# FFN chunks in two-bank tiles of the scan's PSUM ring, and two PSUM banks for the out-projection

## The chip, the cores and the metric

One Trainium2 chip, 8 cores. Each core runs the same program on one of 8 batch rows, with no exchange between cores. The metric is the device time of the slowest core, in microseconds; lower is better. A verdict takes a median over several executions.

## The reference

Per batch row: x is [4096, 1024]. It is normalised, goes through a two-directional state-space scan (16 heads of 128, state 64, a causal convolution of 4 taps before it), and the sum of both directions is projected back; beside it an FFN product with block-quantised operands and a silu gates the result.

```python
xn = _layernorm(x)
zxbcdt = xn @ in_proj_w.T
y_fw = _branch(zxbcdt, ...)                       # conv + silu, SSD scan, * silu(z), rms norm
y_bw = _branch(zxbcdt[:, ::-1, :], ...)
s = (y_fw + y_bw[:, ::-1, :]) @ out_proj_w.T
xq, xs = _mx_quantize(xn); wq, ws = _mx_quantize(weight)    # blocks of 32
g = _silu((xq * xs) @ (wq * ws).T + bias)
x = x + s * g
```

## The kernel before

The row of 4096 tokens is cut into 16 groups of 256 tokens, and a group into 2 chunks of 128. The kernel makes two passes. The first goes through the groups backwards: it projects, runs the backward scan and spills x, B and C, silu(z), y and the quantised xn (sp_x, sp_bc, sp_z, sp_y, sp_xd) to memory. The second, which this change touches, goes forwards and for each group g does:

- `b_scan(g)`: the scan of both chunks, written by `scan_pair`. `weights` makes the decay exponents in a two-bank PSUM tile (TensorE, `ps<-rh,lts`), takes exp of 1024 columns on ScalarE and two products on VectorE (`e`). `outputs` makes y (`ps<-xtm,e`, then `ps<-st,gc`), which VectorE gates with silu(z) (`yz<-ps,sz`). `carry` makes the new state (`ps<-xtm,bw`, then `st`). `factors` makes `gc` and `dec` from the broadcast decays `g`. `norm` makes the rms factor in small operations and scales yz.
- `decays(g + 1)`: the small decay sums of the next group, with the matmuls `ps<-sm,tri` and `ps<-sm,onesf` (one of each a group), a transpose `ltt<-spl`, a store `scr<-ltt` and the loads `rh<-scr` and `g<-scr`.
- `b_out(g - 1, ...)`: the out-projection of the two chunks of the group before; each chunk is two halves of 512 columns, each half two units of 8 matmuls (`ps<-ar,yt`, or `ps<-ar` where the transposed yz lies in `ar`). VectorE multiplies by the FFN gate (`ost<-ps,ar` or `ar<-ps,ar`), GpSimd adds the residual.
- `b_sum(g)`: yz plus the backward y (`yz<-yz,ar` or `yz<-yz,yb`), then its transposes (`yt<-yz`, or `ar<-yz`).
- `b_front(g + 1)`: loads, and `conv_group`, which runs the convolution on TensorE (`ps<-sbc,cd` once and `ps<-stg,cd` x32 for each of four quarters, in one two-bank tile CV), silu on ScalarE (`cvb`, `cvx` x4), the transposes `xtm<-cvx`, and the small product `ps<-cvb` in a tile of PJ.
- `ffn_chunk` for the two chunks of group g: for each half of 512 columns 8 matmuls `ps<-ar,xt` and one for the bias (`ps<-ar,on`), then a silu into gf (`ar<-ps` on ScalarE).

PSUM has 8 banks of 512 columns: `PJ` two of one bank, `CV` one of two banks, `SC` two of two banks. A `Ring` hands its buffers out in turn, in the order in which the code asks; whoever takes one waits for the last reader. Before this change the second pass splits PJ: bank 0 is PO (out-projection), bank 1 is PF (FFN halves and the small product).

The order in which each engine works is not that of the code. `Plan.queues` simulates the program with costs of its own and always picks, among the units of an engine that are ready, the one of lowest rank (its turn). A unit's waits stand before it, but on TensorE `emit` moves a wait that was known early into the last matmuls of the unit ahead (the last four of a short unit, the last two of a long one), so that unit ends late if the awaited thing is late. ScalarE takes its table functions in order of turn: all exp of a turn, then all silu of the next, so there are two table loads a group. Reordering thus follows from any change of rings or costs.

Of the kernel before, what the change touches and what calls it, by code (L numbers as in the profile page):

```python
# [12 lines left out]
AF = mybir.ActivationFunctionType  # L13
# [30 lines left out]
def flat(tokens):  # L44
    for t in tokens:
        if t is None:
            continue
        if isinstance(t, (list, tuple)):
            yield from flat(t)
        else:  # L50
            yield t


class Plan:
# [8 lines left out]
    def put(self, eng, steps, after, us, table=None):  # L63
        if not isinstance(steps, list):
            steps = [steps]
        rank = self.turn if self.rank is None else self.rank
        land = 0.25 if eng == "pe" else 0.12
        self.units.append(Unit(eng, steps, sorted(set(flat(after))), us, land, table, None,
                               self.turn, rank))
        return len(self.units) - 1  # L70

    def dma(self, eng, slot, step, after, kb, us=0.5, rate=180.0, lat=None):
        land = lat or 2.0 + kb / rate
        rank = self.turn if self.rank is None else self.rank
        self.units.append(Unit(eng, [step], sorted(set(flat(after))), us, land, None, slot,
                               self.turn, rank))
        return len(self.units) - 1
# [119 lines left out]
def pe_us(cols):  # L197
    return cols / 2300.0


def act_us(n):
    return 0.18 + n * 0.00083


def dve1(n):
    return 0.16 + n * 0.00104
# [50 lines left out]
def record(nc, dr, A, PS):  # L257
    P = Plan()
    put, dma = P.put, P.dma
# [10 lines left out]
    on3 = A("on3", [128, 128], BF16)  # L270
# [48 lines left out]
    ps = PS("ps", [128, 4096], F32)  # L319
# [9 lines left out]
    PJ = Ring("pj", [ps[:, 0:512], ps[:, 512:1024]])  # L329
    CV = Ring("cv", [ps[:, 1024:2048]])  # L330
    SC = Ring("sc", [ps[:, 2048:3072], ps[:, 3072:4096]])
# [34 lines left out]
    def mm(out, lhsT, rhs, start, stop):  # L366
        return lambda e: e.matmul(out, lhsT, rhs, start=start, stop=stop)  # L367

    def act(out, in_, func, bias=None, scale=None, accum=None):
        kw = {}  # L370
        if bias is not None:
            kw["bias"] = bias
        if scale is not None:
            kw["scale"] = scale
        if accum is not None:
            kw["accum_out"] = accum
        return lambda e: e.activation(out, in_, func, **kw)  # L377

    def tt(out, a, b, op):
        return lambda e: e.tensor_tensor(out, a, b, op=op)  # L380
# [12 lines left out]
    def go(out, in_, **kw):  # L393
        return lambda e: e.dma_start(out=out, in_=in_, **kw)  # L394
# [44 lines left out]
    k_on3 = dma("sp", "k3", go(on3[:], dr["c_on3"]), [k_wz[3]], 32)  # L439
# [626 lines left out]
    for q in range(4):  # L1066
# [18 lines left out]
    wfv = ar[:, WF:WF + 8192].rearrange("p (m k f) -> p m k f", m=8, k=8)  # L1085
    k_wf = dma("sp", "wfl", go(wfv, dr["wf"].rearrange("m p k f -> p m k f")),
               [old, wf_stores], 2048)
# [6 lines left out]
    fbt = ar[:, fb_o:fb_o + 1024]  # L1094
    z_fb = put("pool", lambda e: e.memset(fbt, 0.0), [old], 0.9)
    k_fbt = dma("sp", "k15", go(fbt[0:3, :], dr["fbd"]), [k_fbd, z_fb], 6)
# [6 lines left out]
    for r in (YT, YB, GF):  # L1103
        for i in range(len(r.bufs)):
            r.free[i] = [last_a["wx"]]
    XD = Ring("xdl", [xt[i // 2][:].rearrange("p k t -> p (k t)")[
        :, i % 2 * 1024:(i % 2 + 1) * 1024].rearrange("p (k t) -> p k t", k=8) for i in range(4)])
# [9 lines left out]
    def ffn_chunk(ci):  # L1117
        di, xd_, dfree = XD.take()
        h = dma("sp", f"xdl{di}", go(xd_, dr["sp_xd"][ci]),
                [dfree, spill[ci // 2]["xd"][1 - ci % 2]], 256)  # L1120
        gi, gf, gfree = GF.take()
        evs, ps_ = [], []
        for nh in range(2):
            pi, pj, pfree = PJ.take()
            steps = [mm(pj, xd_[:, k, :], wfv[:, nh * 4:(nh + 1) * 4, k, :], k == 0, False)
                     for k in range(8)]
            steps.append(mm(pj, on3[:], fbt[:, nh * 512:(nh + 1) * 512], False, True))
            p = put("pe", steps, [h, k_wf, k_fbt, k_on3, pfree], pe_us(9 * 512))
            ps_.append(p)
            a = put("act", act(gf[:, nh * 512:(nh + 1) * 512], pj, AF.Silu), [p, gfree],  # L1130
                    act_us(512), table="silu")
            PJ.give(pi, [a])
            evs.append(a)
        XD.give(di, ps_)
        return {"g": (gi, gf, evs)}

    def b_front(g):
# [57 lines left out]
    def b_out(g, sc, ff, c):  # L1195
# [6 lines left out]
        for nh in range(2):  # L1202
            hs_ = slice(nh * 512, (nh + 1) * 512)
            pi, pj, pfree = PO.take()
            p = None
# [6 lines left out]
            m = put("dve", tt(o[:, 0:512], pj, gf[:, hs_], ALU.mult), [p, t_g, ofree], dve1(512))  # L1212
            PO.give(pi, [m])
            mu.append(m)
# [6 lines left out]
        U.give(ui, [t_o])  # L1221
        GF.give(gi, mu)

    PO = Ring("po", [ps[:, 0:512]])
    PF = Ring("pf", [ps[:, 512:1024]])
    PO.free, PF.free = [PJ.free[0]], [PJ.free[1]]
    PJ.bufs, PJ.free, PJ.n = PF.bufs, PF.free, 0
    base = P.turn
    P.rank = base - 0.5
    dcs = {0: decays(0, None, t_par, None)}  # L1230
# [19 lines left out]
    for g in range(NG):  # L1250
        P.turn = base + 2 * g + 2
        front["dc"] = dcs[g]
        scans = b_scan(g, front)
        free_group(front, scans)
        if g < NG - 1:
            P.rank = P.turn - 0.5
            dcs[g + 1] = decays(g + 1, None, t_par, None)
            P.rank = None
        if g:
            for c in range(2):  # L1260
                b_out(g - 1, old_scans[c], ffs[c], c)
        b_sum(g, scans)
        old_scans = scans
        P.turn += 1
        if g < NG - 1:
            front = b_front(g + 1)
        ffs = [ffn_chunk(2 * g + c) for c in range(2)]
# [5 lines left out]
def build_nc():  # L1273
# [27 lines left out]
    def PS(name, shape, dt):  # L1301
        return nc.psum_tensor(name, shape, dt).__enter__()

    plan = record(nc, dr, A, PS)
    order = plan.queues()
    count = plan.count
# [85 lines left out]
```

How the kernel before makes its waits and increments, by code:

```python
    def emit(self, eng, handle, sems, queue):  # L156
        units = [self.units[i] for i in queue]
        early = [[] for _ in units]
        if eng == "pe":
            for n in range(1, len(units)):
                if len(units[n - 1].steps) > 4:
                    early[n - 1] = [w for w in units[n].waits if w[2] < units[n - 1].value]
        for n, u in enumerate(units):
            for w in u.waits:
                if not n or w not in early[n - 1]:
                    handle.wait_ge(sems[w[0]], w[1])
            for k, step in enumerate(u.steps):
                if k == len(u.steps) - (4 if u.us < 1.2 else 2):
                    for w in early[n]:
                        handle.wait_ge(sems[w[0]], w[1])
                last = step(handle)
            last.then_inc(sems[u.slot or u.eng], 16 if u.slot else 1)
# [1136 lines left out]
        @block.sync  # L1311
        def _(eng):
            plan.emit("sp", eng, sems, order["sp"])
            for name, value in count.items():
                eng.wait_ge(sems[name], value)
```

## Time and profile before

| | |
|---|---|
| median of 3 runs | 1570.39 us (1562.2 to 1576.58) |
| profiled execution, its own time | 1570.03 us |
| span of its slowest core (core 3) | 1568.1 us; the others 1537.6 to 1566.1 |
| PE busy | 1280.4 us, 82% of the span |
| VectorE, ScalarE, GpSimd busy | 1051.2, 826.2, 709.7 us (67, 53, 45%) |
| mean granted clock of core 3 | 0.949 |
| chain that ended last | PE 46%, DMA 21%, ACT 11%, issue 9%, DVE 6%, SPq 4% |

Times in the rows are microseconds from the start of the span. PE is TensorE, DVE VectorE, ACT ScalarE, POOL GpSimd, SPq the queue of SyncE, which issues all DMAs of the second pass. A bracket at the end of a row gives the idle time of the engine ahead of it and what ended it. Almost all operations are recorded by one helper line each (matmul L367, activation L377), so the names of the tiles tell them apart. The second pass runs from about 850 us to the end.

### The profile page before, as it was taken

Reading aid. Unit: us, or ns where it says so; the run is one execution under the profiler, and the core shown is the slowest. Engines: PE = TensorE matmul, PEld = TensorE weight load, DVE = VectorE, ACT = ScalarE, POOL = GpSimd, SP = SyncE. Lnnn points to the kernel's source line nnn. Section 1 sums busy time; section 2 is a strip of 40 time slices with the busy share of each in tenths; the row PEclk is TensorE's granted clock in tenths of the full one; section 3 lists DMA queues with packets and bytes.
Section 4 is the critical chain, followed back from the end, with each engine's and each line's share of the span. In section 5 each row is a group of like instructions: output and inputs, shape, how many; then the busy total and the mean of one; then the engine's idle time right before and its main releaser. Section 6 shows DMA issues by size and latency. Waiting matters only on the chain.

```text
span 1568.1 us, 38096 instructions; the slowest of 8 cores (1537.6 to 1568.1 us)
## 1 busy us (share of the span) xinstructions
PE 1280.4 (82%) x13440; PEld 774.8 (49%) x13440; DVE 1051.2 (67%) x1792; ACT 826.2 (53%) x1660; POOL 709.7 (45%) x950
## 2 busy tenths in 40 slices
PE   0577898876998899999996579888888888888896
PEld 0453665553666666666663344444444444444442
DVE  2635788655778887788754776567766667776662
ACT  0225566454566566666664664455555555555541
POOL 2332566534545556665531434444434444343443
PEclk9888999988999999999997599999999999999999
DMA  9793788999777988877679878888878889888872
GB/s 170 133 185 90 177 212 192 142 214 182 162 179 182 200 194 195 167 161 167 176 195 234 209 174 218 220 186 202 213 182 216 203 213 209 201 220 208 201 181 85
DMA packets 434548, 291.92 MB, mean 186 GB/s; under 512 B 312687, under 2 KB 383087, under 8 KB 432826
## 3 DMA queue, kind: packets, MB, share of 16 engines
q1 hardware_dynamic: 431770, 276.62, 76.0%
q0 software_dynamic: 2592, 12.88, 5.2%
q8 instruction: 109, 1.79, 0.5%
q14 instruction: 77, 0.63, 0.2%
HBM read 149.20 MB, written 83.89 MB: 149 GB/s over the span
## 4 chain that ended last, share of the span: by engine, by line
PE 46%; DMA 21%; ACT 11%; issue 9%; DVE 6%; SPq 4%; POOL 0%; DVEq 0%; ACTq 0%; POOLq 0%
PE ps L367 46%; DMA xtm<-cvx 5%; SPq L394 4%; DMA g<-scr 4%; DMA scr<-ltt 3%; ACT L377 3%; DMA xt<-xn 2%; ACT cvx L377 2%; DMA ltt<-spl 2%; ACT e L377 2%; DMA ar<-yz 2%; DVE yz L380 1%; DMA rh<-scr 1%; DMA yt<-yz 1%; ACT ar L377 1%
## 5 line engine op out<-in xcount | busy, mean ns | idle before, releaser
L367 PE MATMUL ps<-ar,xt 128*128 128x512 bf16 (+1 forms) x1792 | 382.8, 358 | 123.9 <-DMA xt<-xn 44.3
L367 PEld LDWEIGHTS ps<-ar,xt 128*128 128x128 bf16 x1792 | 150.4, 99 | 317.7 <-issue 174.3
L367 PE MATMUL ps<-xt,ar 128*128 128x256 bf16 x2176 | 267.2, 279 | 25.5 <-ACT cvx L377 11.1
L377 ACT ACTIVATE cvx<-ps,cbt 128x256 bf16<-128x256 f32 x512 | 200.6, 474 | 164.4 <-PE ps L367 99.5
L380 POOL TENSOR_TENSOR stmp<-st,dec 128x1024 f32<-128x1024 bf16 x64 | 132.0, 2062 | 257.8 <-DVE st L380 113.0
L367 PEld LDWEIGHTS ps<-xt,ar 128*128 128x128 bf16 x2176 | 210.4, 100 | 65.4 <-issue 32.4
L380 DVE TENSOR_TENSOR yz<-ps,sz 128x1024 bf16<-128x1024 f32 x128 | 156.2, 1220 | 48.6 <-PE ps L367 48.1
L377 ACT ACTIVATE sq<-yz 128x1024 bf16<-128x1024 bf16 x128 | 134.9, 1054 | 83.6 <-DVE yz L380 58.4
L367 PE MATMUL ps<-ar 128*128 128x512 bf16 x704 | 167.8, 380 | 10.4 <-DVE rr L384 4.3
L367 PE MATMUL ps<-stg,cd 64*64 64x256 bf16 x4096 | 149.7, 285 | 23.9 <-DMA xt<-xn 6.6
L385 POOL TENSOR_SCALAR rr<-rr 128x1 f32<-128x1 f32 x384 | 120.0, 318 | 86.5 <-DVE rr L385 51.1
L380 DVE TENSOR_TENSOR e<-e,cbm 128x1024 bf16<-128x1024 bf16 x128 | 103.3, 810 | 83.1 <-ACT e L377 80.2
L377 ACT ACTIVATE e<-ps 128x1024 bf16<-128x1024 f32 x128 | 129.7, 1017 | 31.8 <-PE ps L367 31.3
L367 PEld LDWEIGHTS ps<-stg,cd 64*64 64x64 bf16 x4096 | 109.7, 111 | 73.1 <-issue 69.7
L380 POOL TENSOR_TENSOR bw<-btm,w 128x1024 bf16<-128x1024 bf16 x64 | 125.7, 1966 | 42.4 <-DMA btm<-cvb 24.5
L377 ACT ACTIVATE sz<-ps 128x512 bf16<-128x512 f32 x128 | 76.5, 598 | 106.2 <-PE ps L367 105.5
L380 POOL TENSOR_TENSOR xd<-v,qs 128x1024 bf16<-128x1024 fp8e4 x40 | 86.7, 2167 | 98.4 <-DVE v L865 41.6
L367 PE MATMUL ps<-xtm,e 128*128 128x128 bf16 x1024 | 85.0, 226 | 52.1 <-DVE spl L391 17.8
L384 POOL TENSOR_SCALAR u<-u,stats 128x1024 f32<-128x1024 f32 x32 | 93.2, 2913 | 71.3 <-DVE xn L385 30.8
L377 ACT ACTIVATE stg<-ps 128x512 bf16<-128x512 f32 x128 | 75.5, 593 | 86.0 <-PE ps L367 85.4
L367 PEld LDWEIGHTS ps<-ar 128*128 128x128 bf16 x704 | 64.0, 98 | 90.0 <-issue 25.0
L377 ACT ACTIVATE ar<-ps 128x512 bf16<-128x512 f32 x64 | 38.4, 600 | 129.2 <-PE ps L367 114.5
(97 smaller groups left out, 1869.1 us busy)
## 6 DMA issues: line engine op xcount, KB each, us to landing
u<-u SPq DMA_DIRECT2D x54, 512.0 KB, 5.6
sp_x<-stg SPq DMA_DIRECT2D x64, 256.0 KB, 3.1
g<-scr SPq DMA_DIRECT2D x64, 256.0 KB, 5.6
sp_z<-sz SPq DMA_DIRECT2D x32, 512.0 KB, 3.6
sp_y<-yz SPq DMA_DIRECT2D x32, 512.0 KB, 4.7
sz<-sp_z SPq DMA_DIRECT2D x32, 512.0 KB, 4.9
stg<-sp_x SPq DMA_DIRECT2D x60, 259.0 KB, 5.9
out<-u SPq DMA_DIRECT2D x22, 512.0 KB, 3.6
```

Of the source, the lines that this page charges most:

```text
L367: return lambda e: e.matmul(out, lhsT, rhs, start=start, stop=stop)
L377: return lambda e: e.activation(out, in_, func, **kw)
L380: return lambda e: e.tensor_tensor(out, a, b, op=op)
L384: return lambda e: e.tensor_scalar(out, a, s1, None, op0=op0)
L385: return lambda e: e.tensor_scalar(out, a, s1, s2, op0=op0, op1=op1)
L394: return lambda e: e.dma_start(out=out, in_=in_, **kw)
```

## The change

In `ffn_chunk` both halves of a chunk go into one two-bank tile taken from SC, the ring of the scan; one silu of 1024 columns reads it and frees it, where two silus of 512 each freed a bank of PF. A scan takes 10 tiles of SC and a group's two FFN chunks now 2, between the carry of the group's second chunk and the first `weights` of the next group's scan. PF is gone: PO is now PJ itself, so the out-projection has both banks in turn, shared with the small product of `conv_group`.

```diff
         gi, gf, gfree = GF.take()
-        evs, ps_ = [], []
+        si, sp, sfree = SC.take()
+        p = None
         for nh in range(2):
-            pi, pj, pfree = PJ.take()
-            steps = [mm(pj, xd_[:, k, :], wfv[:, nh * 4:(nh + 1) * 4, k, :], k == 0, False)
+            half = sp[:, nh * 512:(nh + 1) * 512]
+            steps = [mm(half, xd_[:, k, :], wfv[:, nh * 4:(nh + 1) * 4, k, :], k == 0, False)
                      for k in range(8)]
-            steps.append(mm(pj, on3[:], fbt[:, nh * 512:(nh + 1) * 512], False, True))
-            p = put("pe", steps, [h, k_wf, k_fbt, k_on3, pfree], pe_us(9 * 512))
-            ps_.append(p)
-            a = put("act", act(gf[:, nh * 512:(nh + 1) * 512], pj, AF.Silu), [p, gfree],
-                    act_us(512), table="silu")
-            PJ.give(pi, [a])
-            evs.append(a)
-        XD.give(di, ps_)
+            steps.append(mm(half, on3[:], fbt[:, nh * 512:(nh + 1) * 512], False, True))
+            p = put("pe", steps, [h, k_wf, k_fbt, k_on3, sfree, p], pe_us(9 * 512))
+        evs = put("act", act(gf[:], sp, AF.Silu), [p, gfree], act_us(1024), table="silu")
+        SC.give(si, [evs])
+        XD.give(di, p)
...
-    PO = Ring("po", [ps[:, 0:512]])
-    PF = Ring("pf", [ps[:, 512:1024]])
-    PO.free, PF.free = [PJ.free[0]], [PJ.free[1]]
-    PJ.bufs, PJ.free, PJ.n = PF.bufs, PF.free, 0
+    PO = PJ
```

What the planner makes of it. TensorE, end of a group in the middle of the second pass, before. `stg,cd` is a quarter of the convolution, `ar,xt` with `ar,on` an FFN half, `rh,lts` the exponents of the next scan, `ar` alone out-projection:

```order
L367 MATMUL ps<-rh,lts1 128x4x64 x8
L367 MATMUL ps<-ar,xt0 128x512 [waits s_act,s_xdl1]
L367 MATMUL ps<-ar,xt0 128x512 x7
L367 MATMUL ps<-ar,on3 128x512
L367 MATMUL ps<-ar,xt0 128x512 [waits s_act]
L367 MATMUL ps<-ar,xt0 128x512 x6
L367 MATMUL ps<-ar,xt0 128x512 [waits s_yt1]
L367 MATMUL ps<-ar,on3 128x512
L367 MATMUL ps<-ar 128x512 x14
L367 MATMUL ps<-ar 128x512 [waits s_act]
L367 MATMUL ps<-ar 128x512
L367 MATMUL ps<-rh,lts1 128x4x64 x4
```

The same place after, in a group whose next chunk's transposed yz has the semaphore s_yt0:

```order
L367 MATMUL ps<-stg1,cd 64x256 [waits s_act,s_rh]
L367 MATMUL ps<-stg1,cd 64x256 x3
L367 MATMUL ps<-rh,lts0 128x4x64 x4
L367 MATMUL ps<-rh,lts0 128x4x64 [waits s_act]
L367 MATMUL ps<-rh,lts0 128x4x64 x3
L367 MATMUL ps<-stg2,cd 64x256 [waits s_act,s_sxl2]
L367 MATMUL ps<-stg2,cd 64x256 x27
L367 MATMUL ps<-stg2,cd 64x256 [waits s_yt0]
L367 MATMUL ps<-stg2,cd 64x256 x3
L367 MATMUL ps<-ar 128x512 x22
L367 MATMUL ps<-ar 128x512 [waits s_act]
L367 MATMUL ps<-ar 128x512
```

The FFN halves have moved ahead of the last two quarters; the wait for the transposed yz has moved from the last FFN half into the last quarter of the convolution; three units of out-projection follow, where two did. Other groups end otherwise. This is the end of the next one after, up to the decays' matmul sm,tri:

```order
L367 MATMUL ps<-stg2,cd 64x256 x32
L367 MATMUL ps<-ar,xt0 128x512 x8
L367 MATMUL ps<-ar,on3 128x512
L367 MATMUL ps<-rh,lts1 128x4x64 x4
L367 MATMUL ps<-stg3,cd 64x256 x32
L367 MATMUL ps<-ar,xt0 128x512 x8
L367 MATMUL ps<-ar,on3 128x512
L367 MATMUL ps<-rh,lts1 128x4x64 x8
L367 MATMUL ps<-sm0,tri 128x32
L367 MATMUL ps<-sm0,onesf 128x32
L367 MATMUL ps<-xtm1,e0 128x128 x8
```

No out-projection stands between its last quarter and the next scan's first xtm,e. Counted from one sm,tri to the next over the 13 intervals in the middle of the pass, the units of out-projection were 8 each, but 10 in the first; after they are 12, 4, 12, 6, 10, 4, 12, 4, 12, 4, 12, 6 and 10.

VectorE, from the broadcast decays to the sums of yz, before (rr scales: the norm):

```order
L384 TENSOR_SCALAR yz1<-yz1,rr0 128x2048 [waits s_pool]
L380 TENSOR_TENSOR gc0<-g,cvb1 128x1024 [waits s_g01,s_g00]
L380 TENSOR_TENSOR yz1<-yz1,ar 128x2048 [waits s_dve,s_ybl0]
L391 CAST dec0<-g 128x8
L380 TENSOR_TENSOR gc1<-g,cvb1 128x1024
L391 CAST dec1<-g 128x8
L384 TENSOR_SCALAR yz2<-yz2,rr1 128x2048 [waits s_pool]
L380 TENSOR_TENSOR yz2<-yz2,yb 128x2048 [waits s_dve,s_ybl1]
```

and after, as in 9 of those 13 groups:

```order
L380 TENSOR_TENSOR gc0<-g,cvb1 128x1024 [waits s_g01,s_g00]
L391 CAST dec0<-g 128x8
L380 TENSOR_TENSOR gc1<-g,cvb1 128x1024
L391 CAST dec1<-g 128x8
L384 TENSOR_SCALAR yz1<-yz1,rr0 128x2048 [waits s_pool]
L380 TENSOR_TENSOR yz1<-yz1,ar 128x2048 [waits s_dve,s_ybl0]
L384 TENSOR_SCALAR yz2<-yz2,rr1 128x2048 [waits s_pool]
L380 TENSOR_TENSOR yz2<-yz2,yb 128x2048 [waits s_dve,s_ybl1]
```

The first norm and the first sum have moved behind both gc products.

## Rows read from the trace of the kernel before

**Rows 1.** Waits of PE, 880 to 1540: total us, times, longest

```profile
PE ps L367 <- ACT ar L377: 30.0, 26, 2.6
PE ps L367 <- DVE spl L391: 17.8, 12, 1.5
PE ps L367 <- DVE sm L380: 16.1, 17, 2.0
```

**Rows 2.** Chain that ended last, second pass: start, us, what

```profile
969.53 1.28 ACT L377
...
1264.87 1.28 ACT L377
...
1290.11 6.95 DMA g<-scr
...
1299.12 6.66 DMA ar<-yz
...
1471.68 1.28 ACT L377
```

**Rows 3.** Busy by window: us, PE, PEld, DVE, ACT, POOL, PEclk, DMA, GB/s

```profile
1300.00:1400.00 100.00, 84.98 (x831) 44.15 (x830) 70.20 (x111) 52.11 (x102) 39.76 (x55) 1.00 0.92 218
```

**Rows 4.** Timeline of PE, one group: start, us, instruction, wait

```profile
1269.80 0.36 PE L367 MATMUL ps<-sm,tri 128*128 128x32 f32 x2
...
1284.77 0.64 PE L367 MATMUL ps<-xtm,bw 128*64 128x128 bf16 x16
...
1300.37 1.89 PE L367 MATMUL ps<-ar,xt 128*128 128x512 bf16 x8 [0.29 <-ACT ar L377]
...
1303.36 1.67 PE L367 MATMUL ps<-ar,xt 128*128 128x512 bf16 x7 [0.89 <-ACT ar L377]
1305.92 0.38 PE L367 MATMUL ps<-ar,xt 128*128 128x512 bf16 x1 [0.88 <-DMA ar<-yz]
...
1311.72 0.49 PE L367 MATMUL ps<-xtm,e 128*128 128x128 bf16 x6 [0.89 <-DVE sm L380]
```

**Rows 5.** Timeline of DVE, the same group

```profile
1297.22 0.69 DVE L380 TENSOR_TENSOR gc<-g,cvb 128x1024 bf16<-128x1024 bf16 x1 [1.62 <-DMA g<-scr]
...
1301.42 2.46 DVE L384 TENSOR_SCALAR yz<-yz,rr 128x2048 bf16<-128x2048 bf16 x1
```

**Rows 6.** Timeline of ACT, the same group

```profile
1298.06 1.57 ACT L377 ACTIVATE cvx<-ps,cbt 128x256 bf16<-128x256 f32 x4 [1.35 <-DMA xtm<-cvx]
...
1306.61 0.60 ACT L377 ACTIVATE ar<-ps 128x512 bf16<-128x512 f32 x1 [3.39 <-PE ps L367]
1307.22 1.28 ACT L377 ACT_TABLE_LOAD   x1
```

**Rows 7.** Groups by form, 880 to 1540: count, busy, mean ns, idle before

```profile
L377 ACT ACTIVATE e<-ps 128x1024 bf16<-128x1024 f32 x64 | 64.9, 1016 | 28.0 <-PE ps L367 28.0
...
L377 ACT ACTIVATE ar<-ps 128x512 bf16<-128x512 f32 x63 | 37.8, 600 | 126.8 <-PE ps L367 112.1 <-DVE ar L380 11.0 <-DVE rr L385 3.6
```

**Rows 8.** Timeline of PE, the end of the kernel

```profile
1540.19 1.89 PE L367 MATMUL ps<-ar,xt 128*128 128x512 bf16 x8 [1.63 <-ACT ar L377]
...
1546.69 3.61 PE L367 MATMUL ps<-ar 128*128 128x512 bf16 x16 [0.94 <-DVE ost L380]
...
1556.01 3.61 PE L367 MATMUL ps<-ar 128*128 128x512 bf16 x16 [1.08 <-DVE ost L380]
```

**Rows 9.** DMA issues, 880 to 1540: median us to landing

```profile
xtm<-cvx SPq DMA_TRANSPOSE x64, 5.9
```

**Rows 10.** Timeline of SP, which issues the DMAs, the same group

```profile
1304.53 1.57 SPq L394 DMA_TRANSPOSE xtm<-cvx  x1
```

**Rows 11.** Busy by window, a short stretch; PEclk is third from the end

```profile
1130.00:1135.00 5.00, 3.18 (x9) 1.01 (x9) 5.00 (x5) 1.41 (x5) 4.05 (x2) 0.75 1.20 282
```

**Rows 12.** Timeline of PE in that stretch

```profile
1131.62 2.76 PE L367 MATMUL ps<-ar,xt 128*128 128x512 bf16 x8 [1.99 <-ACT ar L377]
...
1135.70 3.57 PE L367 MATMUL ps<-ar,xt 128*128 128x512 bf16 x8 [0.89 <-ACT ar L377]
```

## Prediction

> **What bounds the kernel now.** I read the waits of TensorE first, then the chain that ended last, then TensorE, ScalarE and VectorE in order of time over one group of the second pass. In the second pass TensorE waits most often for ScalarE's silu of an FFN half: 30.0 us in 26 waits [rows 1]. That is the single bank: a half can't start before the silu of the half before has read it. Behind it stand the waits for e at the head of a scan, 17.8 and 16.1 us [rows 1].
>
> These waits are not the whole of the bound. The chain shows a table load for exp at 969.53 and again at 1471.68, twelve groups later: (1471.68 - 969.53) / 12 = 41.85 us for a group [rows 2]. TensorE is busy 84.98 of 100 us [rows 3], so a group holds 41.85 x 0.85 = 35.6 us of its work and 6.3 us of gaps. My marker is the small matmul sm,tri, one per group. From the marker at 1269.80 the group goes on so [rows 4]: carry of the second chunk at 1284.77, then the FFN halves, where the ring costs 0.29 and 0.89 us, then 0.88 us for the transposed yz, which landed at about 1305.8, 36.0 us after the marker; then the next scan's first xtm,e at 1311.72. The chain says why yz is that late: the decays' broadcast g lands at 1290.11 + 6.95 = 1297.1, VectorE's product gc waits for it, the sum of yz stands behind gc in VectorE's queue, and its transposes take 6.66 us more [rows 2, 5]. ScalarE's last silu starts at 1306.61 and the table load at 1307.22, so 1.4 us after yz landed; the marker then follows 4.9 us after a table load (1264.87 to 1269.80) [rows 2, 4, 6]. So the ring and the arrival of yz both end the same stretch, within a microsecond.
>
> **The change, part by part.**
>
> *Two silus of 512 columns become one of 1024.* 0.600 us each before; the same read of 1024 columns with exp takes 1.016 [rows 7]. 1.20 - 1.02 = 0.18 us less on ScalarE for each of 32 chunks, 6 us in all. ScalarE is the waiting side there (its silus wait for PE), so I count nothing. If it counted in full it would be 6 us.
>
> *The waits of the ring go.* At most the 30.0 us of [rows 1]. What makes them vanish also lets all four FFN halves run earlier: they no longer stand behind the third and fourth convolution but ahead of them. What took the time under the last transposes, silus and table load is then gone from there.
>
> *Out-projection in two banks.* In the tail the last 64 matmuls no longer wait for VectorE: three waits, the first 0.94 and the last 1.08 us, together 3.0 us [rows 8]. The wait of 1.63 us of the last FFN half [rows 8] goes too, but yz's transposes may be what comes next there; I take 1 us. Tail: -4 us (bounds 0 and -4.7). With two banks the planner also runs out-projections ahead, and unevenly: counted between markers, the 13 intervals of the middle hold 12, 4, 12, 6, 10, 4, 12, 4, 12, 4, 12, 6 and 10 units of 8 matmuls, where before each held 8. A unit is half of 3.61, 1.8 us [rows 8]. So TensorE's work in an interval is 35.6 + 4 x 1.8 = 42.8, 35.6 - 7.2 = 28.4, 32.0 or 39.2 us.
>
> *What moves onto the path.* In 9 of the 13 intervals (all but those with 4 units) the early wait for yz now stands in the last matmuls of the third or fourth convolution, no longer in the last FFN half. There it holds up a convolution, and with it the last silus before the table load. Also, in 9 of 13 groups both gc products, which wait for g, now stand ahead of the first norm of yz on VectorE, in 2 more one of them; before, the norm was ahead of both. A gc is 0.69 us, the slow norm 2.46 [rows 5]. The nearest bounds for yz's landing: 36.0 us after the marker as before (the norms are often late anyway), and 36.0 + 0.7 + 2.5 = 39.2. I take 37.5, nearer the lower end, since the scan with more out-projections in it makes the norms late rather than g.
>
> Each kind of interval then:
> - 12 units: TensorE reaches the wait after 42.8 - 7.8 = 35.0 us of work (behind it stand 4 units and a decay matmul group, 7.2 + 0.6), plus one scan gap of 1.5 (17.8 / 12, [rows 1]) = 36.5. yz at 37.5; 37.5 + 7.8 = 45.3.
> - 10 units: work reaches the wait sooner, yz decides: 45.3.
> - 6 units: again yz decides: 37.5 + 0.1 for the rest of the convolution + 1.6 of silus [rows 6] = 39.2, + 4.9 to the marker = 44.1.
> - 4 units: no wait for yz, but nothing is left to fill the tail. The last convolution ends after some 27.4 us of work + 1.5 + 0.5 for the single conv tile = 29.4, silus 31.0, marker 35.9. Then the first xtm,e of the next scan needs the transposes of the fourth quarter, which start only now: 5.9 us median [rows 9], 36.9, where before they had been issued ahead of the table load. In the crowded stretch they were issued at 1304.53, which is 34.7 after the marker, and so landed near 40.6 at the latest [rows 4, 9, 10]. Between 36.9 and 40.6, leaning to the free queue, I take 38.2.
>
> Sum: 5 x 45.3 + 2 x 45.3 + 2 x 44.1 + 4 x 38.2 = 558.1 against 13 x 41.85 = 544.1: +14.0. With the tail's -4: +10. The profiled execution took 1570.0 us by its own clock, the median of the runs is 1570.4, so both stand together, and I forecast 1570.0 + 10 = 1580 us, the ring's gain eaten by what was hidden under it. Own range of this case 1565 to 1597: lower end with yz at 36.0 again (9 x 1.5 = 13.5 less), upper end with the short intervals at 40.6 (4 x 2.4 = 9.6) and some clock loss.
>
> **Clock.** After TensorE gaps the granted clock falls: 1130 to 1135 shows 0.75, behind a wait of 1.99 us, and the eight matmuls of an FFN half take 2.76 and then 3.57 us where they take 1.89 at full clock [rows 4, 11, 12]. That is 0.9 + 1.7 = 2.6 us for such a stretch at the lower level, 1.2 GHz. The gaps of the short intervals, some 5 us before the marker, invite it; the gaps of the ring do so now. I count these against each other, and leave a surplus to the rivals. The Trainium skill speaks for the change here: "TensorE: Matmul & The Clock Gate", section "A second HAM failure mode: psum-queue depth-cycling", says that small pauses between bursts which cycle through PSUM banks cost clock. The same page's section "HAM oscillation — how this bites in real kernels" speaks against it, since longer waits for transfers between bursts drop the clock each time. The trace agrees with the second, by the rows just named; no row tells the first alone.
>
> **Rivals.**
> - *The ring's waits are the bound, and yz is in time* (chance 0.27). For it: the row of 30.0 us is the largest, and 0.88 us was all that yz cost in the group read. Against: the sum above. Gain at most 30.0 + 4.7 + twice 2.6 = 40; with half of the gaps refilled by others, about 25, so 1545 us.
> - *Slower clearly* (0.23): yz lands at 39.2 instead of 37.5 since gc stands ahead of the norm, and the fourth quarter's transposes land at 40.6. 9 x 1.7 + 4 x 2.4 = 24.9 more, 1605 us, and each short interval may add 2.6 us of clock. This one decides from yz at about 38.5 on. By the skill's section on oscillation alone, a clock loss in every short interval would be 4 x 2.6 = 10 us on top of 1580, which is 1590.
> - The gain of the shorter silu alone, with nothing else moved, would be under 6 us and not be seen.
>
> **How the numbers follow.** About even or a little slower, 1580: 0.50, of which two thirds lie within 1% (1554.7 to 1586.1, about what can be told from no change) and a third above. Fast rival 0.27, nearly all of it faster by over 1%. Slow rival 0.23, with a small part within 1%. So faster 0.25, same 0.38, slower 0.37. Range 1542 to 1612.
>
> **What would show it.** Right: the waits "PE <- ACT ar" near zero; table loads for exp alternating at about 45 and 38 us; PE in a stg convolution waiting for DMA yz or yt; the first xtm,e of a scan waiting for DMA xtm. In the tail, no wait of the last 64 matmuls for VectorE. Wrong: a uniform distance under 40.5 us between table loads, or yz landing less than 36 us after the marker; then the order of the planner did better than I hold. If the clock row falls below 0.9 in many stretches, the slow rival's reason is the clock.

## The result: slower by 3.2%, and where the time lies

The changed kernel takes 1627.0 us (median of 4 runs, 1609.6 to 1630.2) where the kernel before takes 1569.4 (4 runs, 1562.2 to 1576.6): ratio 1.032, 95% interval 1.027 to 1.038. The forecast was 1580 us with a range to 1612, so the direction was right and the size was not. Medians are over all executions of a kernel; ratios leave out those in a slower state, with half of the chip at a lower clock or the whole over 1.5% above the fastest.

The cores of the kernel after show spans of 1585.5 to 1628.4 us, all eight at a granted clock of 0.909 to 0.918; before they stood at 0.944 to 0.956. Cores differ in when the middle of the second pass gets going, by 27 us before and 39 us after. That middle itself repeats far better. I cut each core's time at the marker sm,tri: up to the first marker of the middle, the 13 intervals of the middle, and the rest. The last 14 markers of each core's timeline of PE give these means over the eight cores.

| us, mean of 8 cores | up to the middle | middle, 13 intervals (lowest to highest core) | rest |
|---|---|---|---|
| before | 921.3 | 541.7 (536.1 to 547.3) | 91.3 |
| after | 919.9 | 591.4 (587.9 to 595.1) | 88.2 |

The 49.7 us more in the middle are the whole loss; the end of the kernel gained 3. Core 7, the slowest, also came 26 us late into the middle (946.2 against the mean of 919.9), and the highest span of 1628.4 holds this chance.

Of the page of after, the busy time of the engines and the granted clock in 40 slices:

```profile
PE 1305.7 (80%) x13440; PEld 789.8 (49%) x13440; DVE 1016.5 (62%) x1792; ACT 821.2 (50%) x1628; POOL 720.8 (44%) x950
...
PEclk9777999989999999999996788988999999888999
```

ScalarE has 32 instructions less than before, the merged silus. The later slices of the second pass stand at 8 or 9, where before all were 9.

The waits of PE from 880 to 1590 in after (total us, times, longest), which answer to [rows 1]:

```profile
PE ps L367 <- ACT e L377: 42.1, 13, 7.7
PE ps L367 <- ACT cvx L377: 23.6, 13, 5.2
PE ps L367 <- DVE sm L380: 11.6, 9, 2.6
PE ps L367 <- DMA xtm<-cvx: 11.1, 3, 5.0
PE ps L367 <- DMA ar<-yz: 10.9, 4, 4.2
PE ps L367 <- DMA yt<-yz: 9.5, 4, 3.2
PE ps L367 <- ACT ar L377: 5.8, 2, 4.5
```

The change did what it says: the wait for the silus, 30.0 us in 26 waits before, is down to 5.8 in 2. In its place stand waits for e, for the convolution's evictions cvx, for their transposes xtm and for yz, of which [rows 1] had none among the first three. Those for e and xtm stand mostly behind a group's last convolution, those for cvx ahead of it.

Four windows from marker to marker on core 7, with 12, 4, 12 and 4 out-projection units, and the 100 us that [rows 3] shows of before (us, busy of PE, PEld, DVE, ACT, POOL, then PEclk, DMA share, GB/s):

```profile
1218.20:1268.60 50.40, 45.22 (x395) 22.93 (x396) 29.32 (x48) 21.21 (x41) 19.87 (x27) 0.90 0.89 220
1268.60:1303.40 34.80, 28.02 (x331) 15.40 (x330) 22.88 (x42) 20.67 (x41) 17.21 (x26) 0.91 0.83 186
1303.40:1353.90 50.50, 44.87 (x395) 23.72 (x396) 28.07 (x49) 21.77 (x42) 19.70 (x27) 0.90 0.87 206
1353.90:1396.10 42.20, 29.58 (x332) 16.00 (x330) 26.24 (x44) 20.88 (x40) 16.63 (x26) 0.92 0.74 176
...
1300.00:1400.00 100.00, 79.66 (x744) 42.43 (x743) 59.61 (x106) 48.01 (x93) 36.33 (x52) 0.88 0.83 197
```

An interval with 12 units costs 50.4 us, one with 4 units 34.8 or 42.2. Before, they held 8 units each (the first 10) and took 41.7 us on average. Per 100 us PE is busy 5.3 us less, and at a lower clock.

The timeline of PE in after around the end of the third window shows what the bunching leaves (start, us, instruction, wait):

```profile
1341.20 0.96 PE L367 MATMUL ps<-stg,cd 64*64 64x256 bf16 x28 [1.00 <-ACT cvx L377]
1344.70 0.43 PE L367 MATMUL ps<-stg,cd 64*64 64x256 bf16 x4 [2.54 <-DMA ar<-yz]
1345.06 6.83 PE L367 MATMUL ps<-ar 128*128 128x512 bf16 x24
1351.72 0.60 PE L367 MATMUL ps<-rh,lts 128*128 128x256 bf16 x4
1352.16 1.89 PE L367 MATMUL ps<-ar 128*128 128x512 bf16 x8
1353.89 0.30 PE L367 MATMUL ps<-sm,tri 128*128 128x32 f32 x2
1354.03 0.39 PE L367 MATMUL ps<-sm,onesf 128*128 128x32 f32 x2
1354.25 0.60 PE L367 MATMUL ps<-rh,lts 128*128 128x256 bf16 x4
1358.91 1.01 PE L367 MATMUL ps<-xtm,e 128*128 128x128 bf16 x8 [4.05 <-DMA xtm<-cvx]
1359.71 2.90 PE L367 MATMUL ps<-ar 128*128 128x512 bf16 x8
```

The last convolution ends at 1345.13, and the scan's first outputs (xtm,e) start at 1358.91. In the 13.8 us between them PE has four out-projection units and small work, and waits 4.05 us at the end. The unit behind the gap takes 2.90 us where one takes 1.89 at full clock. Fifty microseconds earlier, at the end of the interval with 4 units, there is no unit of out-projection at all in that place:

```profile
1292.63 1.90 PE L367 MATMUL ps<-ar,xt 128*128 128x512 bf16 x8
1294.36 0.38 PE L367 MATMUL ps<-ar,on 128*128 128x512 bf16 x1
1299.28 1.01 PE L367 MATMUL ps<-rh,lts 128*128 128x256 bf16 x4 [4.53 <-ACT ar L377]
1301.73 1.01 PE L367 MATMUL ps<-rh,lts 128*128 128x256 bf16 x4 [1.44 <-ACT e L377]
1303.42 0.61 PE L367 MATMUL ps<-sm,tri 128*128 128x32 f32 x2 [0.68 <-DVE sm L380]
```

Weights matmuls rh,lts are all that is left, and they need a tile of the scan's ring, which has only two. The first waits until the silu has read the merged FFN tile, the second until e is read.

I call the time from the end of the last convolution's matmuls to the first xtm,e **the bridge**. It is a chain of evictions, transposes and e that PE can't shorten, only fill. Summed from the instructions of PE, means over the 13 bridges of the middle and the eight cores:

| us | last convolution ends, after the marker | bridge | PE busy in it | idle | out-projection units in it |
|---|---|---|---|---|---|
| before | 26.5 | 14.8 | 11.6 | 3.2 | 2.2 |
| after | 36.8 | 12.5 | 8.3 | 4.2 | 2.6 |

The bridge became shorter, but its filling shrank by more: it lost FFN halves, and the out-projection in it is spread unevenly, 4, 1, 3, 2, 4, 1, 5, 0, 4, 1, 3, 2 and 4 units. This is the smaller part of the loss. Over the whole middle PE is busy 489.9 us against 465.6 before (two units more are worth 3.6 of these 24.3 us, the rest are slower matmuls, at a granted clock of 0.89 against 0.98), idle in the bridges 54.3 against 42.1, and idle elsewhere 47.1 against 34.1. And the bridge starts 10 us later in its interval, since units of out-projection now stand ahead of the last convolution.

### The profile page after: what moved, and what is told of

Read it like the earlier page. It is cut to its first block, busy times and chain, and to the rows that moved or that the text cites. A ratio compares the mean times of both kernels' runs of the same rounds, so it can differ in the third digit from the quotient of the medians.

```text
span 1628.4 us, 37988 instructions; the slowest of 8 cores (1585.5 to 1628.4 us)
## 1 busy us (share of the span) xinstructions
PE 1305.7 (80%) x13440; PEld 789.8 (49%) x13440; DVE 1016.5 (62%) x1792; ACT 821.2 (50%) x1628; POOL 720.8 (44%) x950
## 4 chain that ended last, share of the span: by engine, by line
PE 47%; DMA 20%; issue 9%; SPq 8%; DVE 8%; ACT 7%; POOL 1%; DVEq 0%; POOLq 0%; ACTq 0%
PE ps L367 47%; SPq L394 8%; DMA xtm<-cvx 5%; DMA xt<-xn 2%; DMA xd<-xd 2%; DMA u<-u 2%; ACT L377 2%; DVE yz L380 2%; DMA g<-scr 2%; ACT cvx L377 1%; DMA out<-u 1%; DMA ar<-yz 1%; ACT e L377 1%; ACT sq L377 1%; DMA yt<-yz 1%
## 5 line engine op out<-in xcount | busy, mean ns | idle before, releaser
L367 PE MATMUL ps<-ar,xt 128*128 128x512 bf16 (+1 forms) x1792 | 374.4, 354 | 77.5 <-DMA xt<-xn 43.8
L367 PE MATMUL ps<-ar 128*128 128x512 bf16 x704 | 182.4, 410 | 16.3 <-ACT e L377 13.4
L385 POOL TENSOR_SCALAR rr<-rr 128x1 f32<-128x1 f32 x384 | 134.1, 354 | 84.8 <-DVE rr L385 56.1
L380 DVE TENSOR_TENSOR e<-e,cbm 128x1024 bf16<-128x1024 bf16 x128 | 90.8, 713 | 74.8 <-ACT e L377 71.4
L367 PE MATMUL ps<-rh,lts 128*128 128x256 bf16 x512 | 86.3, 301 | 43.1 <-ACT e L377 37.3
L367 PEld LDWEIGHTS ps<-ar 128*128 128x128 bf16 x704 | 68.4, 104 | 104.3 <-issue 45.1
```

The costliest lines, as they stand in the source:

```text
L385: return lambda e: e.tensor_scalar(out, a, s1, s2, op0=op0, op1=op1)
```

## The experiments

The theory that I began with: the loss comes from the **order** that the second out-projection bank lets the planner choose. It runs the units as early as it can, 12 and 4 in turn, and little is left to fill the bridge. Rivals: the **banks** themselves (evictions that hold each other and the small cb tile up, which shares them), the merged **FFN tile** in the scan's ring, the **early wait for yz** on which the prediction built, and the **clock**. Ratios are against the kernel before on the same chip; "middle" is the mean of the eight cores' 13 intervals, as above.

**One part at a time.** e1 keeps the merged FFN tile and gives the out-projection its single bank back:

```diff
-    PO = PJ
+    PO = Ring("po", [ps[:, 0:512]])
+    PF = Ring("pf", [ps[:, 512:1024]])
+    PO.free, PF.free = [PJ.free[0]], [PJ.free[1]]
+    PJ.bufs, PJ.free, PJ.n = PF.bufs, PF.free, 0
```

> The FFN part of the change alone: both halves in a tile of SC with one silu, but the out-projection keeps its one bank. Bunching theory (two out-projection banks let the planner pile 12 and 4 units into alternating groups, and what is left without filler waits and loses clock): the units lie 7 and 9 here, so the time is that of before or better, 1545 to 1572 us. Tile theory (the FFN in the scan's ring is what hurts: the next scan's exponents wait for the FFN's silu, and the halves no longer fill the gaps between the convolutions): 1605 to 1630 us.

Measured: 1563.2 us, ratio 0.989 (0.977 to 1.001), middle 522.3, with 7 to 9 units in nearly every interval. Run again (e8, below), 0.985 (0.978 to 0.991). The first interval alone reaches to no change, the second doesn't: the FFN part alone makes the kernel faster, by 19 us in the middle.

e2 has the other part alone: FFN halves with their own silus as before, and both the halves and the out-projection in the two banks of PJ.

```diff
-    PO = Ring("po", [ps[:, 0:512]])
-    PF = Ring("pf", [ps[:, 512:1024]])
-    PO.free, PF.free = [PJ.free[0]], [PJ.free[1]]
-    PJ.bufs, PJ.free, PJ.n = PF.bufs, PF.free, 0
+    PO = PJ
```

> The other part alone: the ring of two PSUM banks serves out-projection and FFN halves, with silus of 512 columns as before. The planner piles the out-projection here too (units 9 9 9 9 4 9 11 4 12 4 12 4 12). Bunching theory: slow, 1600 to 1630 us, with the slow groups those of 12 units and the ones after them. Tile theory: 1560 to 1575 us.

Measured: 1609.4 us, ratio 1.019 (1.006 to 1.033), middle 567.1, 25 us more than before. Its units go 9, 9, 9, 9, 4, 9, 11, 4, 12, 4, 12, 4, 12, and on core 0 its intervals of 12 units take 47.4 to 50.8 us, those of 4 units 34.9 to 41.3. As the bunching theory had it, the loss comes in with the second bank; and the two parts don't add: -19 and +25 alone, +50 together.

**The early wait.** e4 is the kernel after, but the wait for the transposed yz stands at its own unit and no longer in the last matmuls of the unit ahead of it:

```diff
-                    early[n - 1] = [w for w in units[n].waits if w[2] < units[n - 1].value]
+                    early[n - 1] = [w for w in units[n].waits if w[2] < units[n - 1].value
+                                    and not w[0].startswith("yt")]
```

> The changed kernel, same order on every engine, but the wait for the transposed yz stands at its own out-projection and no longer inside the last matmuls of the unit ahead, which is often a convolution. My prediction's step (this wait holds up the convolution and by it the last silus and the table load) expects a gain: nine of thirteen groups wait about 3 us there, so 10 to 25 us less than the changed kernel, about 1605 us. Bunching theory: the order stays and so does the loss, under 8 us less, 1619 to 1630 us.

Measured: 1631.8 us, ratio 1.034 (1.023 to 1.046), middle 586.0. So the gain of 10 to 25 us that the prediction's step expected did not come; where the wait stands is worth 5 of 50 us at most. That yz is late is not cleared by this. PE waits for it as long as in after, now in the bridge. From 880 to 1590, on e4's slowest core:

```profile
PE ps L368 <- DMA ar<-yz: 11.5, 5, 5.3
PE ps L368 <- DMA yt<-yz: 9.8, 5, 3.7
```

Over the middle, as means of eight cores, these waits are 21.9 us, 23.5 in after and 2.4 before, and the idle time of the bridges grows from 54.3 to 71.8. No run lands yz earlier in after's order.

**Even, but late.** e3 is after with the out-projection held until the scan's first outputs. Every interval then has 8 units, as before, but none lies in the bridge.

```diff
-                p = put("pe", steps, [t_yt, t_wo, pfree, p], pe_us(8 * 512))
+                p = put("pe", steps, [t_yt, t_wo, pfree, p, hold], pe_us(8 * 512))
...
-                b_out(g - 1, old_scans[c], ffs[c], c)
+                b_out(g - 1, old_scans[c], ffs[c], c, scans[0].ys[0])
```

> The changed kernel with one dependency more: the out-projection of a group may not start before the first y of the next group's scan, which spreads it evenly again (8 units in each group). FFN tiles and both banks stay. Bunching theory: 1550 to 1580 us. Tile theory: no better than 1605 us. Against the first, a fear of my own: with no out-projection left between the last convolution and the head of the scan, TensorE stands idle there for some 5 us in every group, which would give 1590 us or more.

Measured: 1659.6 us, ratio 1.048 (1.034 to 1.062); run again as e10, 1.052 (1.039 to 1.066). Middle 612.4 and 610.7: the slowest so far, with 8 units in every interval. The theory's 1550 to 1580 us is missed, and the fear beside it came true. So even intervals don't help while the bridge is empty: 54 of the 71 us that its middle is longer than before's are idle time in the bridges (96.0 against 42.1). Its timeline of PE at a head:

```profile
1325.87 1.07 PE L367 MATMUL ps<-stg,cd 64*64 64x256 bf16 x32 [1.00 <-ACT cvx L377]
1331.27 1.01 PE L367 MATMUL ps<-rh,lts 128*128 128x256 bf16 x4 [4.33 <-ACT e L377]
1332.97 0.61 PE L367 MATMUL ps<-sm,tri 128*128 128x32 f32 x2 [0.69 <-DVE sm L380]
...
1333.81 1.04 PE L367 MATMUL ps<-rh,lts 128*128 128x256 bf16 x4
1337.81 1.01 PE L367 MATMUL ps<-xtm,e 128*128 128x128 bf16 x8 [2.96 <-DMA xtm<-cvx]
```

and ScalarE's at the same head, which says what the wait for e is made of:

```profile
1327.11 1.57 ACT L377 ACTIVATE cvx<-ps,cbt 128x256 bf16<-128x256 f32 x4 [1.48 <-PE ps L367]
1328.69 1.28 ACT L377 ACT_TABLE_LOAD   x1
1329.99 0.23 ACT L377 ACTIVATE sm<-sm 128x32 f32<-128x32 f32 x1
1330.12 1.00 ACT L377 ACTIVATE e<-ps 128x1024 bf16<-128x1024 f32 x1
```

The first two weights units were done by PE ahead of the last convolution. The third wants a scan tile, which is free only once the first e is read out. That exp stands behind the last convolution's four evictions (1.57) and the table load (1.28), so PE idles 4.33 us after a convolution however early everything else was. Behind it the transposes of the same evictions end the wait of 2.96; SyncE issues the last of them only at 1332.83, 4.1 us after these evictions, with a transpose of yz and a load among what stands ahead.

**Order against banks.** e5 has the banks of after and the order of e1. The planner plans with the waits of the single bank; then the waits are worked out anew, in that order, from the two banks in turn. All five engines' queues are instruction for instruction those of e1.

```diff
         for nh in range(2):
...
-            pi, pj, pfree = PO.take()
+            n = out_n[0] + sum(x <= out_n[0] for x in CB_AFTER)
+            out_n[0] += 1
+            pj = PJ.bufs[n % 2]
...
-                p = put("pe", steps, [t_yt, t_wo, pfree, p], pe_us(8 * 512))
+                p = put("pe", steps, [t_yt, t_wo, one_bank[0], p], pe_us(8 * 512))
...
-        return order
+        know = {e: {} for e in ENGINES}
+        count = self.count = {}
+        for i, u in enumerate(self.units):
+            u.after = self.real.get(i, u.after)
+            u.waits, u.seen, u.value = [], {}, 0
+        for i in seq:
+            self.settle(i, know[self.units[i].eng], count)
+        return order
```

(one_bank holds the multiply that read the half before; self.real holds what a unit truly depends on, its tokens and the reader of the bank two uses earlier; CB_AFTER tells how many halves of the out-projection stand ahead of each cb tile.)

> The banks of after (out-projection and the small cb tile share both banks in turn, no wait for the multiply of the unit before), but every engine's instructions in exactly the order of the kernel of the second experiment family, the one with the merged FFN tile and one out-projection bank (1563 us, ratio 0.989): all five queues are the same instruction for instruction, only the waits of the out-projection and of cb are fewer. Theory order (what the second bank costs is the order that it lets the planner choose, 12 and 4 units in turn, with nothing left to run ahead of the scan's head): ratio 0.96 to 1.00, intervals from marker to marker of 38 to 41 us, granted clock over 0.93, the 4 us waits for e gone. Rival bank (two banks shared by out-projection and cb cost time by themselves, for instance because evictions and cb now hold each other up): ratio 1.02 or more, clock under 0.92, as in after.

Measured: 1549.3 us, ratio **0.981 (0.973 to 0.988)**, clock 0.939 to 0.948, middle 516.8. It has the banks and the work of after, in another order, and is 5% faster. The rival "bank" falls, and with it the sharing of the banks with the cb tile: e5 shares them too. Beside it ran e1 again:

> The merged FFN tile with one silu, one bank for the out-projection, again beside e5 on one chip: 0.98 to 1.00 of before; theory order has it within 1% of e5, the rival bank has it 2% or more faster than e5.

Measured: 1555.8 us, 0.985 (0.978 to 0.991), middle 522.6. In the ratios the two can't be told apart. In the stretch behind the last marker, with 23 units in both, e5 takes 87.2 us and e8 91.6: the 4 us that a second bank is worth in the tail are there once the order doesn't take them back.

Two windows of e5 from marker to marker, with 9 and 7 units (core 0):

```profile
1209.70:1249.10 39.40, 36.32 (x376) 19.50 (x378) 28.60 (x46) 21.54 (x41) 17.54 (x26) 1.00 0.97 227
1249.10:1288.70 39.60, 33.25 (x344) 17.80 (x347) 28.59 (x46) 21.49 (x41) 17.44 (x26) 0.95 0.94 220
```

and its bridge, where out-projection units lie between the weights units:

```profile
1242.71 2.07 PE L383 MATMUL ps<-ar 128*128 128x512 bf16 x8
1244.62 0.60 PE L383 MATMUL ps<-rh,lts 128*128 128x256 bf16 x4
1245.05 2.18 PE L383 MATMUL ps<-ar 128*128 128x512 bf16 x8
1247.07 0.60 PE L383 MATMUL ps<-rh,lts 128*128 128x256 bf16 x4
1248.65 0.61 PE L383 MATMUL ps<-xtm,e 128*128 128x128 bf16 x8 [0.98 <-DVE sm L396]
```

In this bridge the waits of 4 us have become one of 0.98; its neighbour with 7 units has waits of 2.06 and 1.85.

**A nudge to the planner instead of a replay.** e6 is after with one wish: a group's second chunk is not projected before the last outputs of the running scan. As e3, but with the anchor

```diff
-                b_out(g - 1, old_scans[c], ffs[c], c)
+                b_out(g - 1, old_scans[c], ffs[c], c, scans[1].ys[1] if c else None)
```

> After, with one wish of order added: the out-projection of the second chunk of a group may not start before the last outputs of the running scan. The planner then puts 9, 8, 9, 8, 8, 7, ... units between the markers instead of 12 and 4, and still has two to four units ahead of the scan's head. Theory order: ratio 0.97 to 1.01 and the wait for e at the head under 2 us in most groups. Rival bank, or that the bunching is not what matters: ratio 1.02 to 1.04 as in after.

Measured: 1572.5 us, ratio 0.993 (0.988 to 0.998), middle 532.5. One added dependency turns 3.2% lost into 0.7% gained. The bet that the wait for e falls under 2 us failed: PE's waits from 880 to 1540 on the slowest core are

```profile
PE ps L367 <- ACT e L377: 33.8, 12, 4.7
PE ps L367 <- DMA xtm<-cvx: 15.3, 9, 3.0
```

so the e and xtm waits are about those of after, and what it regained lies elsewhere. Every kernel so far, sorted by the middle (us, means of eight cores):

| kernel | middle | last convolution ends, after the marker | bridge | PE busy | idle in bridges | idle elsewhere | ratio |
|---|---|---|---|---|---|---|---|
| e5 | 516.8 | 27.3 | 12.7 | 460.5 | 35.0 | 21.3 | 0.981 |
| e1 | 522.3 | 27.5 | 13.0 | 462.1 | 38.9 | 21.2 | 0.989 |
| e6 | 532.5 | 32.6 | 10.8 | 466.7 | 49.7 | 16.2 | 0.993 |
| before | 541.7 | 26.5 | 14.8 | 465.6 | 42.1 | 34.1 | 1 |
| e2 | 567.1 | 34.7 | 12.5 | 484.5 | 42.8 | 39.8 | 1.019 |
| e4 | 586.0 | 35.3 | 13.7 | 487.8 | 71.8 | 26.4 | 1.034 |
| after | 591.4 | 36.8 | 12.5 | 489.9 | 54.3 | 47.1 | 1.032 |
| e3 | 612.4 | 40.9 | 10.5 | 487.0 | 96.0 | 29.3 | 1.048 |

The idle time in the bridges doesn't tell the kernels apart: e6 has nearly as much as after and is 59 us shorter, e2 has before's and is 25 longer. What goes with the middle is how late the last convolution ends. Over 10 us of bridge follow it in each of them, so what stands ahead of it moves the next scan back. In e5 and e1 it ends at 27, in after at 37, in e3, where all 8 units stand ahead of it, at 41. Only before breaks this rank; it alone waits 24.0 us for the FFN's silus. This is read from the traces of eight kernels; no run moves the last convolution and nothing else.

**Is it the clock?** Three kernels put 16 matmuls of 512 columns whose result nobody uses (3.5 us at full clock, 56 us over the kernel) into each scan of e3's kernel. If the low clock behind the gap is what costs, filling the gap should pay.

```diff
+        if t_fill:
+            pi, pj, pfree = PJ.take()
+            w0 = wov[:, 0, :]
+            b.fill = put("pe", [mm(pj, w0[:, 0:128], w0[:, 0:512], k == 0, k == 15)
+                                for k in range(16)], [a.ds[1], a.cg["q_used"], pfree, t_fill],
+                         pe_us(16 * 512))
+            PJ.give(pi, [b.fill])
         b.weights(0)
```

That is e11, behind the last convolution and ahead of the third weights unit. In e7 they stood behind the third weights unit instead; in e9 they lacked the dependency on the convolution (q_used), and the planner put them ahead of it.

> The kernel of the third experiment (two banks, out-projection held until the scan's first outputs; 1659.6 us, clock 0.84 to 0.88, a wait of 4.3 us for e at each head) with 16 matmuls of 512 columns without use put just ahead of each scan's first outputs, into a free bank; 16 times 3.5 us of TensorE work are added, 56 us in all, about 4 us of each of 16 gaps is there to take them. Theory that half of the loss is the clock (the gap lowers the granted clock of the work behind it): the granted clock rises to 0.92 or more, the time falls to 1590 to 1630 although work is added. Rival (the clock is low for another reason, such as the share of weights and transfers, and the wait alone counts): clock stays under 0.89 and the time is 1655 to 1680.

> As e7_fill, but the 16 useless matmuls of 512 columns stand ahead of the third weights unit of the scan, whose wait for the first e (4.3 us, for its PSUM tile) is the gap at the head; in e7 they came behind that wait and could not fill it. Added work 16 times 3.5 us = 56 us, into 16 gaps of about 4.3 us. Theory clock (the head's gap lowers the granted clock of the work behind it): in the intervals of the middle the clock goes from 0.87 to 0.93 or more, an interval loses 2 us or more, and the time falls to 1600 to 1635, below the kernel of e3 on the same chip by 1.5% or more. Rival (the wait itself counts and its filling changes nothing else): clock of the intervals under 0.90, the time within 1% of the e3 kernel. Third (the matmuls do not fit and come out on the path): slower than the e3 kernel by over 1%.

> The kernel of the third experiment again, as the base of e9 on the same chip: 1640 to 1670 us, ratio 1.04 to 1.06, clock of the middle intervals 0.86 to 0.88.

> In e9 the planner put the 16 useless matmuls ahead of the last convolution, because the first two weights units stand there too; the gap behind it stayed. Here they must follow the last convolution and stand ahead of the third weights unit, where the wait for e of 4.3 us is in the kernel of e3 and e10 (1650 and 1660 us, ratio 1.05, clock 0.86). Theory clock: the clock of the middle intervals rises from 0.86 to 0.93 or more, an interval loses 2 us or more against 46.8, ratio 1.00 to 1.03. Rival (the wait itself counts, and its filling changes nothing else): clock under 0.90 and ratio 1.04 to 1.06 with the wait for e gone from the rows, since it is filled. Third (what stands at this place delays the scan all the same): ratio over 1.06.

| kernel | ratio | middle | clock by core |
|---|---|---|---|
| e3 / e10, no filling | 1.048 / 1.052 | 612.4 / 610.7 | 0.887 to 0.904 (e10) |
| e7, behind the wait | 1.079 (1.069 to 1.090) | 654.5 | 0.907 to 0.924 |
| e9, ahead of the convolution | 1.083 (1.067 to 1.099) | 652.8 | 0.898 to 0.911 |
| e11, in the gap | 1.045 (1.036 to 1.053) | 602.3 | 0.928 to 0.937 |

e7 came out beyond both of its ranges, and e9 as its third outcome. They cost (654.5 - 612.4) / 13 = 3.2 us an interval, nearly the whole 3.5. That PE's time is what counts there is not shown: in e7 PE waits for the transposes xtm for 44.5 us of the middle behind the useless matmuls, where e10 has 27.3 (means of eight cores). In the gap they are free and more: (602.3 - 611.5) / 13 = -0.7 us, 611.5 being the mean of e3 and e10. Five intervals each of e10 and of e11 on core 2:

```profile
1108.20:1343.20 235.00, 186.56 (x1785) 100.66 (x1810) 148.92 (x226) 106.71 (x206) 92.28 (x130) 0.86 0.71 186
```

```profile
1103.70:1339.90 236.20, 201.19 (x1890) 104.99 (x1891) 148.65 (x226) 107.42 (x206) 93.33 (x130) 0.93 0.71 185
```

The clock went from 0.86 to 0.93, PE is busy 14.6 us more, and five intervals take the same time within 1.2 us. Where the clock rose is told by one bridge and the stretch up to the next, in e10 and then in e11:

```profile
1195.06:1205.13 10.07, 2.90 (x13) 1.77 (x13) 4.53 (x12) 7.62 (x15) 0.00 (x0) 0.58 0.93 238
1205.13:1242.18 37.05, 34.31 (x345) 18.32 (x350) 25.35 (x33) 13.74 (x26) 18.99 (x26) 0.93 0.62 163
```

```profile
1193.11:1203.32 10.21, 5.35 (x29) 2.60 (x30) 4.53 (x12) 7.80 (x15) 0.00 (x0) 0.95 1.05 271
1203.32:1240.70 37.38, 35.30 (x351) 18.48 (x352) 24.93 (x33) 13.72 (x26) 19.55 (x26) 0.92 0.60 162
```

Over the middle of all eight cores the granted clock of e10 is 0.61 in the bridges and 0.93 outside them, that of e11 0.92 and 0.94. The filling gave the clock back in the 10 us in which PE waits for others anyway. There PE waits less for e (14.9 against 58.6 us) and as long as before for the transposes (31.9 against 27.3), and the bridges together shrink from 131.2 to 128.0. Outside them PE's busy time falls from 450.9 to 446.6 us and the time from 479.5 to 474.3.

So the time came out as the rival "the wait counts" had it, and the clock as the clock theory had it. The Trainium skill, "TensorE: Matmul & The Clock Gate", section "HAM oscillation — how this bites in real kernels", says that waits between bursts drop the clock at each burst; the rows agree, 0.58 in the bridge with the gaps and 0.95 with them filled. What a low clock costs outside the bridges, where PE is busy nearly all the time, e11 can't tell, since it hardly changed it. After has 0.75 in the bridges and 0.95 outside, before 0.98 and 0.98.

## Why the prediction was off

- **The ring's waits go: right.** 30.0 us became 5.8. "What took the time under the last transposes, silus and table load is then gone from there" was the right sentence, and the loss is in it; the sum priced it in the intervals of 4 units only.
- **Silu merge: right.** 1.02 us for 1024 columns as taken; no run has it alone. But the merged tile brought 1.1% in e1 and 1.5% in e8. PE's waits for the FFN's silu fall there from 24.0 to 10.8 us of the middle and those for e rise from 3.6 to 11.8 (e1, means of eight cores), so the freed FFN halves, which the fast rival had for its reason, are a part of these 19 us and not shown to be all.
- **Tail, -4 us: right.** 91.3 to 88.2 for all behind the last marker, and 91.6 to 87.2 in e8 and e5 where the units in it are as many. The last 64 matmuls now run in one piece:

```profile
1603.84 0.38 PE L367 MATMUL ps<-ar,xt 128*128 128x512 bf16 x1 [2.14 <-DMA ar<-yz]
...
1604.43 15.49 PE L367 MATMUL ps<-ar 128*128 128x512 bf16 x64
```

  against 17.5 us with three waits before, of which [rows 8] shows two. The wait of 2.14 for yz in front of them is what the prediction said might come next.
- **The intervals.** On core 7, means by kind:

| units | predicted | measured | how many |
|---|---|---|---|
| 12 | 45.3 | 51.2 | 5 |
| 10 | 45.3 | 44.9 | 2 |
| 6 | 44.1 | 47.3 | 2 |
| 4 | 38.2 | 38.5 (32.5 to 44.5) | 4 |

  The sum is 594.5 against 558.1, and 29.6 of the 36.4 us are in the intervals of **12 units: the step that failed**. It took 42.8 us of work at full clock and one scan gap of 1.5, let yz come at 37.5, and added 7.8 us up to the next marker. Measured, those intervals have 43.1 to 45.4 us of busy time at a clock of 0.88 to 0.94 and 2.8 to 11.6 us of gaps. Over the eight cores their last convolution ends at 38.5 to 42.2 us, 40.7 on average, in place of 37.5, and what follows takes 9.6 in place of 7.8, since waits for e stand there and the sum had none. Together these make 50.4 where the sum has 45.3. In three of the five PE waits for yz in the last convolution, until 38.1, 41.9 and 41.0; in the other two it doesn't, and the convolution ends as late. The 4-unit mean was right by luck, as a mean of two kinds: 32.5 and 34.8, and 42.2 and 44.5 where the head waits 4.0 and 5.0 us for xtm.
- **yz at 37.5 after the marker:** 41.3 in the group shown (1344.70 - 1303.42), beyond my upper bound of 39.2, and between 34.8 and 41.9 where PE waits for it. That the wait's place inside a convolution is what costs was wrong: e4 takes it out and the middle takes 586.0 us in place of 591.4. Whether yz's lateness costs is open, for PE's waits for it stayed.
- **The waits of 17.8 us** that I put at the head of a scan end inside it (one at 1278.34, 8.5 us behind its marker). The sum used them as a gap of 1.5 in the scan, so it doesn't change.
- **The clock "against each other":** false as a statement of the clock, which fell from about 0.95 to 0.92 over the kernel and from 0.98 to 0.89 in the middle. The extra busy time of the middle, 489.9 against 465.6 us, holds 3.6 of two more units and about 21 of slower matmuls, which looks like half of the loss. It says little of the time: a part of it lies in the bridges, where e11 gave the clock back and little time with it. What share of after's own 50 us the clock holds is open; no run raised its clock and left its order alone.
- **The signs** that I named came: waits for yz inside a convolution, a scan's first xtm,e waiting for xtm, and nearly no wait for the silus. So the kinds of waits were foreseen and their size in the long intervals was not; the slow rival's 1605 us was nearer, and still too low.

What stays open besides: why the parts add up to more than their sum (-19 and +25 against +50). The order of after differs from e5's in many places at once, and no run prices the moved FFN halves, the late convolutions and the uneven units one by one. And whether a better order than e5's exists for these banks wasn't tried.

## What to carry to other kernels

A buffer added for a greedy planner or scheduler is also a change of order: look where the work that it lets go early used to be, what latency it covered there, and what it now stands ahead of. To tell a resource from an order, give the new resource the old order (e5); here that turned +3.2% into -1.9%. Price a moved unit by the chain of fixed length that it holds up or leaves unfilled, as much as by the wait that it no longer has.

## What I had not expected of the hardware

- The mean granted clock of TensorE is a poor guide to the time here. It went from 0.86 to 0.93 when 4 us gaps were filled with useless matmuls, and the 47 us interval became 0.7 us shorter. What rose was the clock of the gaps' own stretch, from 0.61 to 0.92, where other engines set the pace; outside it stood at 0.93 and 0.94.
- The same 3.5 us of useless matmuls cost 3.2 us an interval on either side of a wait and nothing in it. Between a last convolution and the next scan stand evictions (1.57), a table load (1.28), an exp (1.0) and transposes, whatever TensorE does: no kernel had a mean bridge under 9.8 us.
- A part of a program that no edit touched (up to the first marker of the middle) differs between cores of one execution by up to 39 us (907.2 to 946.2 in after), while the 13 intervals that follow agree within 7.2. A single slowest-core time mixes the two; the stretch that the edit touches, taken on all cores, told the kernels apart far more sharply than the ratios did.
